# Four instructions of 512 columns in place of one of 2048 on VectorE, in the shared-expert stages of a hybrid layer kernel

## What is computed

```python
x = x + attn_a(layernorm(x), ...)   # S4D long convolution, then a layer norm
x = x + ffn(layernorm(x), ...)      # experts
x = x + attn_b(layernorm(x), ...)   # causal attention, 16 heads of 8, ALiBi
x = x + ffn(layernorm(x), ...)      # experts, the same weights
```

```python
logits = xf @ gate_w + gate_b
top_w, top_i = top_k(logits, 2); gw = softmax(top_w)
for e in range(8):                  # hidden width 512
    h = gelu(xf @ w1[e] + b1[e])
    out = out + combine[:, e:e+1] * (h @ w2[e] + b2[e])
shared = gelu(xf @ ws1 + bs1) @ ws2 + bs2
```

## Time and profile before

| | |
|---|---|
| median of 3 executions | 877.78 us (877.6 to 879.66) |
| the profiled execution | 878.74 us |
| its span, first to last instruction | 877.0 us |
| TensorE busy | 630.6 us, 72% |
| VectorE busy | 637.9 us, 73% |
| ScalarE busy | 444.6 us, 51% |
| GpSimd busy | 460.7 us, 53% |
| mean granted clock of TensorE | 0.889 of full speed |

### The profile page before, as it was taken

How to read it: one execution, slowest core, us unless ns; L and a number is a source line. 1 busy time by engine, 2 the same in 40 slices (tenths; PEclk the granted TensorE clock), 3 DMA queues, 4 the chain that set the end, 5 groups by cost and what they waited for, 6 DMA issues and landing times.

```text
span 877.0 us, 21902 instructions
## 1 busy us (share of the span) xinstructions
PE 630.6 (72%) x7826; PEld 467.8 (53%) x7826; DVE 637.9 (73%) x1395; ACT 444.6 (51%) x873; POOL 460.7 (53%) x567
## 2 busy tenths in 40 slices
PE   0197974793079999324799998998975797999940
PEld 0073431563069998212466665665542566998940
DVE  6989997683058888387678777787743974888846
ACT  5642157761045555271766666675663243555524
POOL 1126776887757777510002131554568881777760
PEclk9977998897589999755799999999996998999985
DMA  9510001326144464242121323232212413444417
GB/s 286 144 38 0 1 0 37 76 60 105 53 70 86 90 98 87 90 160 61 44 81 53 90 64 93 63 110 77 63 30 55 80 35 56 91 86 95 100 34 273
DMA packets 131849, 70.50 MB, mean 80 GB/s; under 512 B 89535, under 2 KB 118725, under 8 KB 131746
## 3 DMA queue, kind: packets, MB, share of 16 engines
q1 hardware_dynamic: 121042, 50.46, 24.5%
q0 software_dynamic: 9088, 16.88, 7.1%
q10 hardware_dynamic: 1616, 1.77, 0.7%
HBM read 26.61 MB, written 30.50 MB: 65 GB/s over the span
## 4 chain that ended last, share of the span: by engine, by line
POOL 30%; PE 22%; issue 19%; DVE 15%; SPq 5%; ACT 4%; DMA 4%; POOLq 1%; DVEq 0%; ACTq 0%
POOL expert_out_g L1391 7%; POOL slots L1032 7%; POOL slots L1045 7%; DVE ARENA L2144 3%; PE banks L1868 3%; POOL expert_out_f L1391 3%; PE banks L1884 2%; PE banks L1401 2%; PE banks L1941 2%; SPq L1116 2%; PE banks L1403 2%; SPq L1770 2%; PE banks L1861 2%; PE banks L1402 2%; PE banks L1846 1%
## 5 line engine op out<-in xcount | busy, mean ns | idle before, releaser
L1440 ACT ACTIVATE ARENA<-banks,ARENA 128x256 f32<-128x256 f32 x312 | 122.0, 474 | 151.9 <-PE banks L1403 136.1
L2144 DVE TENSOR_REDUCE ARENA<-banks 128x4 f32<-128x1024 f32 (+1 forms) x128 | 122.8, 959 | 45.7 <-PE banks L1884 44.5
L1401 PE MATMUL banks<-ARENA,W1H 128*128 128x256 f16 x312 | 87.1, 279 | 50.9 <-DMA ARENA<-slots 43.5
L2066 ACT ACTIVATE ARENA<-banks 128x1536 f32<-128x1536 f32 x64 | 92.8, 1450 | 58.6 <-PE banks L1912 58.6
L1415 PE MATMUL banks<-W2L,ARENA 128*128 x624 | 110.6, 219 | 2.9 <-DVE ARENA L1453 2.5
L1472 DVE CAST ARENA<-ARENA 128x1024 f16<-128x1024 f32 x78 | 60.6, 777 | 70.4 <-ACT ARENA L1440 66.6
L1417 PE MATMUL banks<-W2H,ARENA 128*128 x624 | 110.0, 219 | 0.0
L1416 PE MATMUL banks<-W2H,ARENA 128*128 x624 | 110.0, 219 | 0.0
L1391 POOL DMA_INDIRECT expert_out_g<-ARENA x78 | 82.8, 1062 | 42.7 <-issue 24.6
L1391 POOL DMA_INDIRECT expert_out_f<-ARENA x78 | 81.2, 1040 | 35.2 <-issue 25.6
L1474 DVE TENSOR_TENSOR ARENA<-ARENA 128x1024 f16<-128x1024 f32 x78 | 95.6, 1225 | 2.7
(11 more groups left out here) (312 smaller groups left out, 1806.8 us busy)
## 6 DMA issues: line engine op xcount, KB each, us to landing
spread<-ARENA SPq DMA_DIRECT2D x96, 64.0 KB, 2.1
ARENA<-expert_out_f SPq DMA_DIRECT2D x8, 512.0 KB, 7.2
ARENA<-spread SPq DMA_DIRECT2D x16, 256.0 KB, 3.0
ARENA<-spread SPq DMA_DIRECT2D x32, 128.0 KB, 3.0
ARENA<-expert_out_g SPq DMA_DIRECT2D x8, 512.0 KB, 4.5
XT<-in_w SPq DMA_DIRECT2D x10, 256.0 KB, 7.7
slots<-EMPTY SPq DMA_DIRECT2D x16, 129.0 KB, 4.6
ARENA<-in_w SPq DMA_DIRECT2D x8, 256.0 KB, 6.6
```

The lines of the kernel that those rows point to most:

```text
L1401: pe.matmul(out, t.W1H[:, e, ms], XST[i][:, 0], start=True, stop=False)
L1440: ins = nc.scalar.activation(HF[i % 2][:, m], UP[i % 2][:, m], ACT.Gelu, bias=BIAS[i % 4][:, m:m + 1], scale=1.0 / WS)
L2144: dve.tensor_reduce(MX[:, G // 2, tile, :, :, G % 2].rearrange("p s a -> p a s"), src, AX.X, ALU.max).then_inc(m_red.sem, 1)
```

## The change

Five instructions of VectorE become several, over the same elements in the same order. The semaphore is raised by the last of them only. Nothing else is touched: neither the waits nor the order of the steps.

```diff
@@ front_stage
         def row_lows(g):
             s = tiles_of(g)
             dve.wait_ge(row_high.sem, row_high.base + g + 1)
-            tt_(ROWS[:, s, D:2 * D], XN[:, s, :], ROWS[:, s, 0:D], ALU.subtract).then_inc(rows_set.sem, 1)
+            for half in (slice(s.start, s.start + GRP // 2), slice(s.start + GRP // 2, s.stop)):
+                ins = tt_(ROWS[:, half, D:2 * D], XN[:, half, :], ROWS[:, half, 0:D], ALU.subtract)
+            ins.then_inc(rows_set.sem, 1)
...
         def split_step(g):
             dve.wait_ge(down_mm.sem, down_mm.base + g + 1)
             dve.wait_ge(high.sem, high.base + g + 1)
-            tt_(H16[:, g % 2, 1], HF[:, g % 2], H16[:, g % 2, 0], ALU.subtract).then_inc(split.sem, 1)
+            for i in range(MT):
+                ins = tt_(H16[:, g % 2, 1, i], HF[:, g % 2, i], H16[:, g % 2, 0, i], ALU.subtract)
+            ins.then_inc(split.sem, 1)
@@ shared_stage
         def split_step(g):
             dve.wait_ge(down_mm.sem, down_mm.base + g + 1)
             dve.wait_ge(hidden.sem, hidden.base + MT * g + 2 * MT)
-            dve.tensor_copy(H16[:, g % 2, 0], HF[:, g % 2]).then_inc(high.sem, 1)
+            for i in range(MT):
+                ins = dve.tensor_copy(H16[:, g % 2, 0, i], HF[:, g % 2, i])
+            ins.then_inc(high.sem, 1)
             dve.wait_ge(high.sem, high.base + g + 1)
-            dve.tensor_tensor(H16[:, g % 2, 1], HF[:, g % 2], H16[:, g % 2, 0], ALU.subtract).then_inc(split.sem, 1)
+            for i in range(MT):
+                ins = dve.tensor_tensor(H16[:, g % 2, 1, i], HF[:, g % 2, i], H16[:, g % 2, 0, i], ALU.subtract)
+            ins.then_inc(split.sem, 1)
```

## The result

| | before | after |
|---|---|---|
| median, executions | 877.96 us (5) | 870.79 us (5) |
| lowest and highest | 877.6 and 879.66 us | 868.08 and 873.77 us |
| the profiled execution | 878.74 us | 868.08 us |
| its span | 877.0 us | 866.4 us |
| granted clock of TensorE | 0.889 | 0.889 |

The ratio of the medians is 0.9912, its 95% interval 0.9891 to 0.9933: faster, by 7.2 us where 13.3 was forecast. The median lies 0.3 us above the range; the range was laid from a median before of 877.78, and 0.9912 of that is 870.1, just inside it. The profiled execution was the shortest of the five and shows 10.7 us. So two things must be told apart: what the change does in that execution, and why the other four are 2.5 to 5.7 us longer.

A forecast was written before the change was run, and what follows sets the result against it. GpSimd's sends, held by long VectorE instructions, were taken to bound two stretches. Front stage 11.0 us (11.7 less 0.7) plus second stage 2.3 gave 13.3, so 865.4 profiled and 864.5 median; range 860.5 to 870.5 us.

The forecast's parts named there:

- GpSimd gets in between two instructions of VectorE: Both stretches of sends: GpSimd's send gets in between back-to-back VectorE instructions although no wait stands between them.
- (b): Both stages: VectorE does not hand over between pieces, a send stands still for the whole series; 882.5 us, chance 0.05.
- (c): Second shared expert: a send in the gap holds VectorE for its whole 0.96 us; 881.6 us in all, chance 0.03.
- the 2.76 us: Front stage: a four-piece series if each instruction waits for an emptied pipeline, 4 x 0.69; the prediction took 2.49.
- A second send of the same series ... loses next to nothing: Front stage: a second send starts 0.83 + 0.30 us after a release, just before another, so costs almost nothing.
- the residue of 1.8 us: Front stage: hold time that stays, about 0.2 us for each of nine series, taken off 13.5 to give 11.7.
- The rows' subtraction, 0.7 us: Front stage, L795 in halves: GpSimd's sum gets in between and delays the path 0.7 us, bounds 0 and 1.3.
- VectorE's price in the front stage is covered: Front stage: eight series 0.20 us longer each, covered because TensorE was done 38.3 us before the routed experts.
- The second stage gives 2.3 us: Second shared expert: 0.8 us from an earlier TensorE start plus 1.5 from its clock; between -2 and 5.
- VectorE's price was put at 2.4 us: Second shared expert: four steps that count cost 0.6 us more each, so the last merge ends at 729.8.
- The fast clock was taken: Routed experts after the second shared expert: TensorE at 2.4 GHz behind a 2.0 us gap, saving 1.5 us, bounds 0 and 2.
- Rival (a): Second stage gives back: GpSimd enters nearly every gap, a step costs 1.2 us, slow clock; 869 us, chance 0.13.

The follow-up runs named there:

- the changed kernel again: The changed kernel unaltered, run once more against the kernel before on another chip: 873.04 us (8 executions), ratio 0.9943.
- the front stage alone: Only the front stage's pieces, casts and subtractions of the second shared expert whole as before, against the kernel before: 870.39 us, ratio 0.9902.

## Why the prediction was right in direction and too large

- **GpSimd gets in between two instructions of VectorE**: right. Holds of the front stage fell from 14.8 to 3.4 us (profiled) and 3.6 to 6.9 us in the other traces. Rivals (b) and (c) are out: what (b) describes holds for one series in eight, and the eight series took 2.48 to 2.63 us in each trace of the changed kernel, so that no send kept VectorE out for its 0.96 us. So the lock that the Trainium skill describes (SBUF — State Buffer, section "Who interferes with whom") is kept by VectorE's instruction to its end, and not by the send: the series of 163.76 took 2.48 us although a send got in. The eight series also rule out the 2.76 us that the prediction worked out by the drain. The Trainium skill, VectorE: DVE Perf Modes, section "The DRAIN you can't avoid", itself adds that a next instruction which is not held starts earlier, and the prediction left this out.
- **"A second send of the same series ... loses next to nothing"**, and with it the residue of 1.8 us: this is the step that failed. It took half a gap as the mean for first sends and nothing for second ones. In the other traces first sends often begin just behind the start of a series and lose 0.5 us. The next send then comes 1.85 us into the series, just before a gap as the prediction has it, but too late for that gap, and loses 0.5 as well. And one series of eight, the seventh, was counted as handed over and was not: 1.6 to 2.3 us. So the changed kernel again and the front stage alone save 9.0 and 8.3 us on sends where 11.7 was forecast (of 14.8 us of holds in all, of which the prediction counted 13.5). The profiled execution saved 11.4, because its sends met the series at better points: that the forecast of 11.7 fits there is luck of the execution.
- **The rows' subtraction, 0.7 us**: right, 0.56 us in every trace. The front stage as a whole gave 10.8 us in the profiled execution (11.0 forecast), and 5.9 to 8.3 by the start of the routed experts in the two traces of the changed kernel again and in that of the front stage alone.
- **VectorE's price in the front stage is covered**: right, 26.2 us of idle TensorE are left.
- **The second stage gives 2.3 us**: wrong, and the second failed step. It is the sum of four terms. (1) VectorE's price was put at 2.4 us. The last merge starts 57.9 us after the first up in place of 55.2; of these 2.7 us, 1.6 are the slow last down, so the pieces themselves cost 1.1 (1.3 to 1.8 in the other three traces with all steps in pieces), less than forecast. (2) That slow down was not in the sum at all: I had the waits of 1.76 us and 3.69 us before me, lengthened the first by 0.4, and asked for the clock only behind the next gap. (3) Behind the merge TensorE needs 721.41 - 719.42 = 2.0 us to load its tables (1.8 to 2.0 over all traces where no load is waited for), not 1.2. The prediction read VectorE's 1.81 us of idle time as three loads. But VectorE's first load begins beside the last merge, at 718.75 (at 726.68 before), and only two fall into the idle time; a load takes 0.6 us and the next starts some 0.85 behind its start. (4) The fast clock was taken, for 1.5 us (bounds 0 and 2). It was high for 0.2 us of the routed experts and then 1.2 GHz (0.42 us for a matmul of 256 columns). The size fits: in the five traces in which the clock stayed high, the part behind is 1.2 to 1.5 us shorter than before. The condition does not hold, since the same gap was followed by either clock. Something of it came nevertheless: from the first matmul to the first scatter it takes 11.3 us in place of 12.1 (10.3 at the fast clock), and the clock is low until 3.7 us behind the first matmul in place of 5.4. Rival (a) comes nearer by its number (869), but only half by its mechanism: the slow clock came, and no step cost 1.2 us. That the range of the prediction just holds the result rests on this rival's bound, and is luck in that measure.
- **The last send**: it ends 42.4 us behind the first up of that stage, against 54.4, and nothing needs it there. The load was the limit for 4.4 us only, as the prediction said; the new limit took these back.
- **The time**: by the profiled execution, 10.7 us for 13.3. The front stage is 0.2 of the difference and the second 2.4: it gave back 0.4, of which the ramp behind it returned 0.3, in place of a gain of 2.3. By the medians it is 7.2, and 5.8 and 6.4 where the changed kernel ran again: about half of the forecast. For 2.4 to 3.1 of the further 3.5 us the traces show a place, the points at which the sends meet the series (holds of 5.8 and 6.5 us in place of 3.4). But both other traces of the changed kernel are of its shortest executions (870.12 and 869.53), so what makes the median of 873 is not shown.

**A better version.** Waits between the pieces of the front stage, and pieces in steps 3 to 6 alone of the second shared expert, gave 865.13 and 866.72 us, ratios 0.9866 and 0.9857: 13 us under the kernel before, and 6.7 us under the changed kernel on the same chip (873.38). Of the two edits the second alone was measured too (868.71 and 870.71 us), the waits alone were not.

**What stays open.** Why the seventh series hands nothing over without a wait; what delays the landing that GpSimd's iota waits for; which clock TensorE gets behind a gap of 2.6 us; what other numbers of pieces than four would give, which was not run; and the rest of the spread over executions, of which the attention stage has a part (305.2 to 308.8 us from the last scatter before it to the first up behind it, in kernels that are the same there).

## What to carry to other kernels

Where GpSimd issues indirect DMAs on the path and VectorE runs long elementwise instructions that have slack, cut those into pieces: a send then loses less than a piece and not the whole. Put a wait between the pieces where VectorE has the time, since without one the hand-over can be missed for a whole series. Cut nothing on a stretch where VectorE itself sets the end, and when a wait of TensorE grows by a few tenths, ask for the clock at that very wait, not only at the next. And when an idle time is read as the price of some work, look whether the work began before the idle time did.

## What the runs showed of the hardware that was not expected

- Sends pass between back-to-back pieces, and the series grows from 2.48 to 2.63 us at most; but in one place a series of four keeps a send out to its end every time. Three waits of 0.12 us each end that.
- Pieces of 512 columns start 0.60 us apart and take 0.69, so four take 2.49, also with sends between them.
- TensorE's granted clock stayed high for the 2.9 us of the last down after waits of 1.75 and 1.76 us (nine traces); after 1.93 us (one) and 2.16 or 2.17 us (four) it fell to 1.2 GHz during the down, which took 4.4 and 4.5 us. After gaps of 2.56 to 2.59 us it stayed high in five traces and fell in four.
- Loading two tables of expert numbers takes TensorE 1.8 to 2.0 us; a load is 0.6 us, and the next starts some 0.85 us behind it.
